# Delta-rule transformer block on one core: the first transfers dealt over two queues, weights prepared in four slices

## What is computed

```python
# layer 0, attention: a delta rule over 1024 steps, width 128
q = x @ Wq + bq;  kr = x @ Wk + bk;  k = kr / max(norm(kr), 1e-12);  v = x @ Wv + bv
alpha = sigmoid(x @ Wa + ba);  beta = sigmoid(x @ Wb + bb);  gate = sigmoid(x @ Wg + bg)
S = a * (S - b * (S k) k^T) + b * v k^T          # per step
o = (q S) * g;  return o @ Wo + bo
...
x = _layernorm(x + _L0_attn_ref(...))
x = _layernorm(x + _L0_ffn_ref(...))             # 3 blocks of two 4-bit quantised linears with LoRA
x = _layernorm(x + _L1_attn_ref(...))
x = _layernorm(x + _L1_ffn_ref(...))             # low-rank MLP
```

## Time and profile before

| | |
|---|---|
| median of 3 runs | 2464.26 us (2462.11 to 2464.99) |
| profiled execution, its own time | 2464.13 us |
| profiled execution, span from first to last instruction | 2462.4 us |
| mean granted TensorE clock | 0.993 |
| PE busy | 2390.5 us, 97% of the span |
| DVE, ACT, POOL busy | 68%, 47%, 27% |
| DMA | 166.26 MB, mean 68 GB/s |

### The profile page before, as it was taken

The page is one execution under the profiler, slowest core; times in us unless marked ns, Lnnn a source line. Parts: engine busy times, 40 slices in busy tenths (PEclk is TensorE's granted clock), DMA queues, the critical chain, the costliest instruction groups (busy, mean ns, idle before and its releaser), DMA issues.

```text
span 2462.4 us, 37382 instructions
## 1 busy us (share of the span) xinstructions
PE 2390.5 (97%) x12333; PEld 1953.3 (79%) x12333; DVE 1669.4 (68%) x3164; ACT 1167.9 (47%) x2225; POOL 676.8 (27%) x1097
## 2 busy tenths in 40 slices
PE   6999999999979999999999999999999999999997
PEld 5878787787867888888888888888888878888886
DVE  3677777767787666676666666666666676666666
ACT  3333333333434334434334343343534477777775
POOL 2223323232340121111211112111021135555555
PEclk9999999999989999999999999999999999999999
DMA  5121212122250020010201102010021223333322
GB/s 134 51 70 37 99 68 102 34 102 85 87 175 1 1 103 1 35 68 8 94 0 53 49 17 85 0 68 34 17 85 47 85 90 111 114 117 115 103 85 69
DMA packets 100654, 166.26 MB, mean 68 GB/s; under 512 B 18356, under 2 KB 21428, under 8 KB 100468
## 3 DMA queue, kind: packets, MB, share of 16 engines
q1 hardware_dynamic: 96560, 163.69, 19.7%
q10 hardware_dynamic: 4036, 1.84, 0.3%
HBM read 115.18 MB, written 50.33 MB: 67 GB/s over the span
## 4 chain that ended last, share of the span: by engine, by line
PE 67%; DVE 1%; POOL 1%; issue 0%; ACT 0%; POOLq 0%; DVEq 0%
PE quant_bank L1487 7%; PE quant_bank L1488 7%; PE quant_bank L1489 7%; PE quant_bank L1877 6%; PE quant_bank L1879 6%; PE quant_bank L1878 6%; PE quant_bank L1514 5%; PE quant_bank L1515 5%; PE quant_bank L1516 5%; PE quant_bank L1504 3%; PE quant_bank L1533 2%; PE quant_bank L1535 2%; PE quant_bank L1534 2%; PE quant_bank L1894 1%; PE quant_bank L1545 1%; PE quant_bank L1476 1%
## 5 line engine op out<-in xcount | busy, mean ns | idle before, releaser
L1356 ACT ACTIVATE quant_g_hi<-quant_bank,kept_beta,kept_gamma 128x512 fp32r<-128x512 f32 x192 | 150.3, 783 | 395.8 <-PE quant_bank L1504 395.8
L1328 POOL TENSOR_SCALAR quant_var<-quant_mv 128x1 f32<-128x1 f32 x256 | 56.7, 221 | 1006.9 <-DVE quant_mv L1403 1006.9
L1487 PE MATMUL quant_bank<-kept_W_hi,quant_h_hi 128*128 128x512 f32 x768 | 305.7, 398 | 0.3 <-DVE quant_h_lo L1392 0.3
L1488 PE MATMUL quant_bank<-kept_W_lo,quant_h_hi 128*128 128x512 f32 x768 | 303.8, 396 | 0.0
L1489 PE MATMUL quant_bank<-kept_W_hi,quant_h_lo 128*128 128x512 f32 x768 | 303.7, 395 | 0.0
L1401 DVE BATCH_NORM_STATS2 quant_stats<-quant_bank 128x6 f32<-128x512 f32 x192 | 133.9, 698 | 195.2 <-PE quant_bank L1489 195.2
L1842 DVE TENSOR_TENSOR mlp_g_lo<-quant_bank,mlp_g_hi 128x512 fp32r<-128x512 f32 x256 | 176.3, 689 | 105.2 <-ACT quant_bank L1779 105.2
L1778 ACT ACTIVATE mlp_g_hi<-quant_bank,mlp_b 128x512 fp32r<-128x512 f32 x256 | 177.2, 692 | 71.2 <-PE quant_bank L1879 63.8
L1514 PE MATMUL quant_bank<-quant_g_hi,kept_W_hi 128*128 128x512 f32 x512 | 205.5, 401 | 0.0
L1515 PE MATMUL quant_bank<-quant_g_hi,kept_W_lo 128*128 128x512 f32 x512 | 202.8, 396 | 0.0
L1516 PE MATMUL quant_bank<-quant_g_lo,kept_W_hi 128*128 128x512 f32 x512 | 202.7, 396 | 0.0
(11 more groups left out here) (283 smaller groups left out, 5940.6 us busy)
## 6 DMA issues: line engine op xcount, KB each, us to landing
delta_x_in<-L_attn_x_d SPq DMA_DIRECT2D x16, 1024.0 KB, 9.4
delta_x_res<-L_attn_x_d SPq DMA_DIRECT2D x16, 1024.0 KB, 7.6
x_d<-delta_z SPq DMA_DIRECT2D x16, 1024.0 KB, 5.1
kept_x_in<-x_d SPq DMA_DIRECT2D x16, 1024.0 KB, 5.4
quant_y<-x_d SPq DMA_DIRECT2D x16, 1024.0 KB, 5.0
x_d<-quant_y SPq DMA_DIRECT2D x16, 1024.0 KB, 4.3
mlp_x_in<-x_d SPq DMA_DIRECT2D x16, 1024.0 KB, 10.4
mlp_x_res<-x_d SPq DMA_DIRECT2D x16, 1024.0 KB, 6.6
```

The costliest lines, as they stand in the source:

```text
L1356: nc.scalar.activation(g_hi[m][:, k, :], tr[k][:, :], ACT.Gelu, bias=beta[:, b, k:k + 1], scale=gamma[:, b, k:k + 1])
L1487: mm(out, x_hi, W_hi[2 * b][:, k, :], start=False, stop=False, skip_group_check=True)
L1488: mm(out, x_hi, W_lo[2 * b][:, k, :], start=False, stop=False, skip_group_check=True)
```

## The change

The transfers of the start are dealt out over both queues. ACT starts only Wq, Wk, Wv, Wg. SP starts, in order: the identity, bq, bk, bv, bg, batch 0 of x by itself (256 KB, semaphore `x_row_in`), ba, bb, batches 1 to 3 of x (768 KB), Wa, Wb, Wo, bo; then it waits for `w_in` (now 4 transfers) and for the new `w_rest_in` (Wa, Wb, Wo) before the masks.

ACT loads a table and runs a 128x4 Sigmoid into `rstd`, whose result nobody reads, before it waits for weights. It copies the 512 projection columns in four slices of 128x512, and DVE makes `w_lo` in four slices behind them; PE's proj(0) waits per slice. Wa, Wb and Wo are prepared later: ACT copies them behind `xT(3)` of the first unit, DVE makes their parts at its piece `ab.0` of the first unit, and PE's `attn` gets the wait for `wo_lo`. PE transposes batch 0 of x as soon as `x_row_in` is there.

```diff
@@ -405,8 +405,21 @@
         @block.sync
         def _(sp):
             sp.dma_start(ident4[:, :, :], consts[:, 0:GB * P].rearrange("p (s n) -> p s n", s=GB)).then_inc(s_["consts_in"], 16)
-            sp.dma_start(x_in[0][:, :, :], rows(x, 0, 0)).then_inc(x_in_dma[0], 16)
-            sp.wait_ge(s_["w_in"], 16 * 7)
+            at = 0
+            for name in ("bq", "bk", "bv", "bg"):
+                size = w[name].shape[0]
+                sp.dma_start(b_all[:, at:at + size], w[name].unsqueeze(0).to_broadcast([P, size])).then_inc(s_["b_in"], 16)
+                at += size
+            sp.dma_start(x_in[0][:, 0:1, :], rows(x, 0, 0)[:, 0:1, :]).then_inc(s_["x_row_in"], 16)
+            for row, name in enumerate(("ba", "bb")):
+                sp.dma_start(b_ab[row:row + 1, :], w[name].unsqueeze(0)).then_inc(s_["b_in"], 16)
+            sp.dma_start(x_in[0][:, 1:, :], rows(x, 0, 0)[:, 1:, :]).then_inc(x_in_dma[0], 16)
+            for j, name in enumerate(("Wa", "Wb")):
+                sp.dma_start(w_st[:, :, PROJ + j:PROJ + j + 1], w[name].rearrange("(k p) c -> p k c", p=P), allow_slow_non_contiguous=True).then_inc(s_["w_rest_in"], 16)
+            sp.dma_start(wo_st[:, :], w["Wo"]).then_inc(s_["w_rest_in"], 16)
+            sp.dma_start(bo_all[:, :], w["bo"].unsqueeze(0).to_broadcast([P, dim])).then_inc(s_["bo_in"], 16)
+            sp.wait_ge(s_["w_in"], 16 * 4)
+            sp.wait_ge(s_["w_rest_in"], 16 * 3)
             sp.dma_start(mask[:, :, :], masks.rearrange("p (l n) -> p l n", l=LEVELS)).then_inc(s_["mask_in"], 16)
             for g in range(1, GROUPS):
                 sp.dma_start(x_in[g][:, :, :], rows(x, 0, g)).then_inc(x_in_dma[g], 16)
...
@@ -567,20 +580,11 @@
         def _(act):
             for j, name in enumerate(("Wq", "Wk", "Wv", "Wg")):
                 act.dma_start(w_st[:, :, j * P:(j + 1) * P], w[name].rearrange("(k p) c -> p k c", p=P)).then_inc(s_["w_in"], 16)
-            for j, name in enumerate(("Wa", "Wb")):
-                act.dma_start(w_st[:, :, PROJ + j:PROJ + j + 1], w[name].rearrange("(k p) c -> p k c", p=P), allow_slow_non_contiguous=True).then_inc(s_["w_in"], 16)
-            act.dma_start(wo_st[:, :], w["Wo"]).then_inc(s_["w_in"], 16)
-            at = 0
-            for name in ("bq", "bk", "bv", "bg"):
-                size = w[name].shape[0]
-                act.dma_start(b_all[:, at:at + size], w[name].unsqueeze(0).to_broadcast([P, size])).then_inc(s_["b_in"], 16)
-                at += size
-            act.dma_start(bo_all[:, :], w["bo"].unsqueeze(0).to_broadcast([P, dim])).then_inc(s_["bo_in"], 16)
-            for row, name in enumerate(("ba", "bb")):
-                act.dma_start(b_ab[row:row + 1, :], w[name].unsqueeze(0)).then_inc(s_["b_in"], 16)
-            act.wait_ge(s_["w_in"], 16 * 7)
-            nc.scalar.activation(w_hi[:, :, :], w_st[:, :, :], ACT.Copy).then_inc(s_["w_hi_done"], 1)
-            nc.scalar.activation(wo_hi[:, :], wo_st[:, :], ACT.Copy).then_inc(s_["w_hi_done"], 1)
+            act.wait_ge(s_["filled"], 1)
+            nc.scalar.activation(rstd[:, :], minus_half[:, :], ACT.Sigmoid)
+            act.wait_ge(s_["w_in"], 16 * 4)
+            for k in range(KT):
+                nc.scalar.activation(w_hi[:, k, 0:PROJ], w_st[:, k, 0:PROJ], ACT.Copy).then_inc(s_["w_hi_done"], 1)
             act.wait_ge(s_["b_in"], B_IN)
             act.wait_ge(s_["bank_written"], 2)
 
@@ -598,6 +602,10 @@
                 act.wait_ge(s_["xT_ps"], GB * (GROUPS * c + g) + s + 1)
                 nc.scalar.activation(xT_hi[:, s, :, :], tr4[s % 2], ACT.Copy).then_inc(s_["xT_hi_done"], 1)
                 seed(c, g, s)
+                if isinstance(c, int) and (c, g, s) == (0, 0, GB - 1):
+                    act.wait_ge(s_["w_rest_in"], 16 * 3)
+                    nc.scalar.activation(w_hi[:, :, PROJ:], w_st[:, :, PROJ:], ACT.Copy).then_inc(s_["w_hi_done"], 1)
+                    nc.scalar.activation(wo_hi[:, :], wo_st[:, :], ACT.Copy).then_inc(s_["w_hi_done"], 1)
 
             def square(c, g, s):
                 n = GROUPS * c + g
@@ -671,12 +679,9 @@
         @block.vector
         def _(dve):
 
-            dve.wait_ge(s_["w_hi_done"], 2)
-            nc.vector.tensor_tensor(w_lo[:, :, :], w_st[:, :, 0:PROJ], as_f32(w_hi[:, :, 0:PROJ]), ALU.subtract).then_inc(s_["w_lo_done"], 1)
-            dve.wait_ge(s_["w_ab_zero"], 1)
-            nc.vector.tensor_copy(w_ab[:, :, 0:2], w_st[:, :, PROJ:]).then_inc(s_["w_ab_done"], 1)
-            nc.vector.tensor_tensor(w_ab[:, :, LO_ROW:], w_st[:, :, PROJ:], as_f32(w_hi[:, :, PROJ:]), ALU.subtract).then_inc(s_["w_ab_done"], 1)
-            nc.vector.tensor_tensor(wo_lo[:, :], wo_st[:, :], as_f32(wo_hi[:, :]), ALU.subtract).then_inc(s_["w_lo_done"], 1)
+            for k in range(KT):
+                dve.wait_ge(s_["w_hi_done"], k + 1)
+                nc.vector.tensor_tensor(w_lo[:, k, :], w_st[:, k, 0:PROJ], as_f32(w_hi[:, k, 0:PROJ]), ALU.subtract).then_inc(s_["w_lo_done"], 1)
 
             settled = (s_["filled"], FILLED)
             dve.wait_ge(*settled)
@@ -688,6 +693,11 @@
 
             def ab_(c, g, _):
                 if isinstance(c, int) and (c, g) == (0, 0):
+                    dve.wait_ge(s_["w_ab_zero"], 1)
+                    dve.wait_ge(s_["w_hi_done"], KT + 2)
+                    nc.vector.tensor_copy(w_ab[:, :, 0:2], w_st[:, :, PROJ:]).then_inc(s_["w_ab_done"], 1)
+                    nc.vector.tensor_tensor(w_ab[:, :, LO_ROW:], w_st[:, :, PROJ:], as_f32(w_hi[:, :, PROJ:]), ALU.subtract).then_inc(s_["w_ab_done"], 1)
+                    nc.vector.tensor_tensor(wo_lo[:, :], wo_st[:, :], as_f32(wo_hi[:, :]), ALU.subtract).then_inc(s_["w_lo_done"], 1)
                     dve.wait_ge(s_["mask_in"], 16)
                     nc.vector.tensor_copy(mask_f32[:, :, :], mask[:, :, :]).then_inc(s_["mask_f32_done"], 1)
                 dve.wait_ge(s_["ab_low_done"], GROUPS * c + g + 1)
@@ -863,7 +873,9 @@
             def xT(c, g, s):
 
                 n = GROUPS * c + g
-                if s == 0:
+                if isinstance(n, int) and n == s == 0:
+                    pe.wait_ge(s_["x_row_in"], 16)
+                elif s == 0 or isinstance(n, int) and n == 0 and s == 1:
                     pe.wait_ge(x_in_dma[g], 16 * c + 16)
                 if s >= 2:
                     pe.wait_ge(s_["xT_lo_done"], GB * n + s - 1)
@@ -874,12 +886,12 @@
             def proj(c, g, s):
 
                 n = GROUPS * c + g
-                if isinstance(n, int) and n == s == 0:
-                    pe.wait_ge(s_["w_lo_done"], 2)
                 pe.wait_ge(s_["xT_hi_done"], GB * n + s + 1)
                 pe.wait_ge(s_["seeded"], GB * n + s + 1)
                 out, cols = p_pj[s % 2][:, :], slice(0, PROJ)
                 for k in range(KT):
+                    if isinstance(n, int) and n == s == 0:
+                        pe.wait_ge(s_["w_lo_done"], k + 1)
                     mm(out, xT_hi[:, s, k, :], w_hi[:, k, cols], start=False, stop=False, skip_group_check=True)
                     mm(out, xT_hi[:, s, k, :], w_lo[:, k, cols], start=False, stop=False, skip_group_check=True)
                 pe.wait_ge(s_["xT_lo_done"], GB * n + s + 1)
@@ -1056,6 +1068,8 @@
             def attn(c, g, s):
 
                 n = GROUPS * c + g
+                if s == 0:
+                    pe.wait_ge(s_["w_lo_done"], KT + 1)
                 pe.wait_ge(s_["ogT_lo_done"], n + 1)
                 if s >= 2:
                     pe.wait_ge(s_["z_done"], GB * n + s - 1)
```

More of the change, by code:

```diff
@@ L254, in delta_rule_and_weights @@
         p_ab = p_tr[0][:, 0:2 * GB].rearrange("p (s z) -> p s z", z=2)
-        names = """consts_in mask_in w_ident w_in b_in bo_in res_done w_hi_done w_lo_done w_ab_zero w_ab_done ab_low_done ab_sum_done bank_written seeded filled
+        names = """consts_in mask_in w_ident w_in w_rest_in x_row_in b_in bo_in res_done w_hi_done w_lo_done w_ab_zero w_ab_done ab_low_done ab_sum_done bank_written seeded filled
             xT_ps xT_hi_done xT_lo_done ab_ps ab_row_done abT_ps row_zero proj_ps sq_done floor_done proj_done ab_done rn_done kbv_done
@@ L443, in load_la @@
                     sp.dma_start(st[i * RANK:(i + 1) * RANK, :, :], q["lora_a"][layers].rearrange("l r d -> r l d")).then_inc(w_[arrived], 16)
-            sp.wait_ge(s_["w_hi_done"], 2)
-            sp.wait_ge(s_["w_lo_done"], 2)
+            sp.wait_ge(s_["w_hi_done"], KT + 2)
+            sp.wait_ge(s_["w_lo_done"], KT + 1)
             sp.wait_ge(s_["w_ab_done"], 2)
```

## The result

Six runs of the changed kernel took 2472.3 us median (2470.81 to 2475.77), six of the kernel before 2464.05 (2462.11 to 2466.35): a ratio of 1.0035, 95% interval 1.0025 to 1.0045. **The change makes the kernel slower by 8.3 us.** The profiled execution took 2470.89 us.

A forecast was written before the change was run, and what follows sets the result against it. PE, busy 97% of the span, was taken to bound the kernel, so only its waits could shorten: -4.3 us at the start and +0.9 ahead of `ab` gave -3.4, from 2464.13 to 2460.7 us; 8-in-10 range 2458.0 to 2464.3.

The forecast's parts named there:

- slower: Whole kernel: the outcome of being slower by over 0.2%, meaning over 2469.2 us; chance 0.02.
- When the weights land: Start: the four wide weights land at 11.8 us, bounds 10.5 and 16.0.
- the +0.9 for the biases: Start: four biases, 256 KB ahead on SP's queue, share the engines with the weights and delay their landing 0.9 us.
- ACT and DVE behind it: Start, behind the weights: six ACT operations take 3.1 us, PE starts at 15.0; DVE's slices cost nothing.
- PE starting as early as 12: Start: the case in which DVE's slices lose their cover and would cost up to 1 us.
- First term: Start: PE begins the first projection at 15.0 instead of 19.33, -4.3 us.
- The second table load: At 25.45 us, during proj(1): the load disappears, with zero gain, below 0.1 us either way.
- What moved in ahead of `ab`: Ahead of `ab`: preparing `w_ab` makes PE start at 31.0 instead of 30.09, +0.9 us.
- Rival A: At `ab`: the longer wait costs PE's clock, 1.8 to 2.5 us more, about 2462.8 us; chance 0.22.
- The clock in proj(0): First projection: runs at 1.2 GHz as before, term 0, bounds -2.3 and +0.8 us.
- C: Start: biases hold up both queues, weights land at 16.0, kernel 2464.8 us; chance 0.07, half case 0.13.
- D: Start: Wo or Wa land late, standing last on SP's queue; chance 0.01.

The follow-up runs named there:

- e2: The changed kernel with `w_lo` made by one DVE instruction again, behind the four slices of `w_hi`: 2476.1 us, ratio 1.0055.
- e3: The changed kernel with 28 more small writes on DVE ahead of its first wait: 2462.74 us, ratio 0.9995.
- e4: The changed kernel with PE's new wait ahead of `attn` kept only in the very first unit: 2472.66 us, ratio 1.0036.
- e8: The changed kernel with Wa, Wb and Wo copied by ACT behind `xT(1)`, their other preparation and the masks' cast on POOL: 2458.69 us, ratio 0.9978.
- e9: The kernel of e8 without the small Sigmoid up front: 2459.17 us, ratio 0.9984.
- e10: The kernel of e8 with the four biases behind the rest of x on SP's queue: 2459.77 us, ratio 0.9983.
- e11: The kernel of e8 with one `w_hi` and one `w_lo` instead of four slices: 2460.66 us, ratio 0.9983.
- e7: The kernel before with twenty 128x1 memsets more on DVE ahead of its first wait: 2475.15 us, ratio 1.0041.

## Why the prediction was wrong

- **The step that failed** is in the first paragraph: "over 2400 us the kernel is as long as PE's work, the change leaves that work alone, and only a stretch in which PE waits can shorten". It could also lengthen, in DVE's loop, whose instructions the diff doesn't touch. The sum had no term for DVE's additional instructions ahead of the loop beyond their durations; that term measured +13.1 us in the profiled pair, of which some 1.5 are the clock's fall behind the fourth jump back. The order of DVE's instructions, shown above the prediction, held the four that mattered (three slices more, and one that the two waits added), but not what they do to the loop behind them. The sum of the rest, 2464.13 - 4.4 = 2459.7, lies inside the range; none of the rivals was this one, and "slower" had 0.02.
- **When the weights land**: forecast 11.8 with a lower bound of 10.5, 10.11 in the profiled run, below the bound. The kernels e2 to e4 and e8 to e11 put it at 10.4 to 11.9, so 10.11 was a good draw, and the +0.9 for the biases remains unshown.
- **ACT and DVE behind it**: 3.1 us to the end of the first seed was right (10.11 to 13.27). PE then started 0.5 us later than that, because I had costed the early transposes at nothing: those of batch 1 stand in front of proj(0) and waited for the rest of x until 12.98. "PE starting as early as 12" didn't come, and DVE's slices hid as argued. First term: -5.6 instead of -4.3.
- **The second table load**: forecast "zero gain, below 0.1"; e9 bounds it at 0.3 us. The load was 1.28 us in both places, as in the row. The Trainium skill ("ScalarE: Activation LUTs", What ACT_TABLE_LOAD costs) has 2.66 us with a drain; the trace shows no drain behind the load.
- **What moved in ahead of `ab`**: +0.9 forecast, the wait grew from 1.78 to 2.62 us, +0.84, ended by `w_ab` as named.
- **Rival A** came true inside this: after 2.62 us of waiting the clock was 0.50 during `ab`. The lead fell from 6.1 at 24 to 3.9 at 35; less the 0.84, that is 1.4 us for the clock where 1.8 to 2.5 were worked out. It was no certainty: the clock fell behind 2.62 us of waiting in the changed kernel, e2 and e3 and stayed in e4, and it stayed behind the 1.78 us in all ten kernels that wait so long there (before and those built on it, e8 to e11). So the forecast's argument, that 2.7 us is nearer to 1.78 than to 3.6, settled nothing, and with one profiled execution of each kernel no rate can be given.
- **The clock in proj(0)** was at 1.2 GHz as taken. **C** and **D** did not happen: Wo landed at 13.8 (issue 7.80 plus 6.0), and ACT came for it at 23.57.

## What to carry to other kernels

Before costing an edit as "a few instructions in an idle stretch", look whether the engine has a hardware loop behind it: the place of its body in that engine's program can decide over microseconds per iteration (shown here for DVE alone). In the profile this looks like idle time ended by "issue" at the first instruction of each iteration (in e7 a few instructions later), with a count of instruction packets that has grown by a multiple of the jumps back; in a new kernel it is tested with one, 4 and 30 harmless instructions ahead of the loop. And when work must move, look for the engine that is idle there: on POOL, and on ACT two batches earlier, the preparation of Wa, Wb and Wo cost nothing, where ACT and DVE just ahead of `ab` had cost PE 0.84 us of waiting and, where the clock fell, 1.4 us more.
